# Attention with a ring of three PSUM banks for turned scores and turned results, TensorE and the DMA queue without loops

## The chip, the cores and the metric

The kernel runs on one core of a Trainium2 chip. The core has five engines with a queue each: TensorE (PE in the profile, its weight loads PEld), VectorE (DVE), ScalarE (ACT), GpSimd (POOL) and SyncE (SP), which here only issues DMAs. They meet through semaphores. PSUM is the memory that TensorE writes: 8 banks of 128 partitions x 512 float32. The metric is the device time of one execution in microseconds (us).

## The reference, cut to what matters

The input `x` is (8 batches, 1024 rows, 256 columns). The first stage, a selective scan with a layer norm, is not touched by the change. The second stage is this, per batch:

```
qkv = (x @ W_qkv + b_qkv).reshape(B, S, 3, 16, 16)         # 16 heads of 16 columns
q, k, v = qkv[:, :, 0], qkv[:, :, 1], qkv[:, :, 2]
attn = softmax(einsum('bqhd,bkhd->bhqk', q, k) / sqrt(16), axis=-1)
attn_out = einsum('bhqk,bkhd->bqhd', attn, v).reshape(B, S, 256)
gate = softmax(x @ W_gate + b_gate)                         # 8 experts, the two best count
expert_out = einsum('bsd,edf->bsef', x, W_experts) + b_experts
moe_out = einsum('bsef,bse->bsf', expert_out, combine)
x = layernorm(x + attn_out + moe_out)
```

## The kernel before

The kernel has two phases. The scan phase takes the first 1880 us. The attention phase goes through the 8 batches; for each batch there are 16 heads (`heads`) and then the experts of the next batch (`experts`), in which the maxima of heads 0 and 1 and the layer norm of the batch before are worked in.

The softmax needs each query's greatest score first. So each head's scores are computed twice. The *scores* (`scores`, L1244) have queries on the partitions; VectorE reduces a tile of 128 queries x 1024 keys to its negated maximum (`take_max`, L1588), in tiles qt = 0 to 7. They go to two pairs of banks, 0-1 and 2-3. The maxima are split in a high and a low half (`split_max`), TensorE turns them into rows (`turn_max`, L1253), ScalarE copies them (`take_max` there, L1476) to `m_rows`, and SyncE writes them by four DMAs into two extra rows of the stacked queries (`max_rows`, L1165). The *turned scores* (`scores_t`, L1261) have keys on the partitions and the maximum already subtracted, by those rows. For each tile kt of 128 keys there are two of 512 queries. ScalarE takes the exponential of each (`exp_unit`, L1463) into `probs`, and TensorE multiplies these with the values, four tiles later (`weigh_v`, L1274, accumulated over the tiles in bank 6). ScalarE copies the sums (`take_o`, L1470), TensorE turns them (`turn_o`, L1286), and VectorE divides by the row sum (`normalise`, L1595 and L1597).

The order on each engine is written out by hand. In `step`, TensorE does for each kt: turned scores half 0, scores of head h + 2 (half 1), turned scores half 1, scores of head h + 2 (half 0), then the value product; behind kt = 3 `turn_max` of head h + 1, behind kt = 6 `turn_o` of head h - 1. Heads 14 and 15 have no scores of a later head; TensorE does the projections of the next batch there (`qk_proj`, L1306). VectorE normalises head h - 1 behind reduction 7 of each step.

Banks: turned scores half 0 go to bank 4 and half 1 to bank 5, so each waits for the exponential of the tile before. Bank 7 holds turned maxima and turned results in turn, guarded by `s_nm` (normalised) and `s_mr` (rows taken). Experts use banks 4, 5 and 6 from their ninth unit on (`EBANK`), and the last two units are 30 (bank 4) and 31 (bank 5).

TensorE runs `heads(b)` and `experts(b + 1)` in a hardware loop of 7 passes; the last `heads` stands behind it. SyncE has a loop over batches with one over heads within it. ScalarE's and VectorE's instructions are written out without loops. SyncE stores a batch's output (`store_out`) in the pass of that batch, and the next pass begins with the rows of head 0.

Of the kernel before, what the change touches and what calls it, by code (L numbers as in the profile page):

```python
# [20 lines left out]
ALU = mybir.AluOpType  # L21
# [940 lines left out]
def attention_phase(nc, d):  # L962
    with ExitStack() as ctx:
# [152 lines left out]
        TERMS = tuple((k, w, x) for k in range(KH) for w, x in ((0, 0), (0, 1), (1, 0)))  # L1116
        block = ctx.enter_context(nc.Block())

        @block.sync
        def _(sp):  # L1120
# [68 lines left out]
            with sp.Fori(0, HEADS) as h:  # L1189
# [43 lines left out]
        def _(pe):  # L1233
# [15 lines left out]
            def turn_max(b, h, normalised):  # L1249

                pe.wait_ge(s_nm, normalised + 1)
                pe.wait_ge(s_mp, b * HEADS + h + 1)
                pe.transpose(ps[0:2 * TT, 7, 0:P], m_parts[:, :, :].rearrange("p c t -> p (c t)"), ident[:, :]).then_inc(s_mt, 1)  # L1253

            def scores_t(b, h, kt, half):
# [4 lines left out]
                pe.wait_ge(s_p, g * (2 * TT) + (2 * kt + half + 1))  # L1260
                pe.matmul(ps[:, 4 + half, :], head(k_st, half, QM, h, kt * P, P),  # L1261
# [16 lines left out]
            def turn_o(b, h, turned=False):  # L1278
# [44 lines left out]
            def step(b, h, before, ahead, front):  # L1323
# [3 lines left out]
                for kt in range(TT):  # L1327
# [8 lines left out]
                    if turned and kt == 3:  # L1336
                        turn_max(b, h + 1, b * HEADS + h - 1 if before else b * HEADS)
                    if before and kt == 6:
                        turn_o(b, h - 1, turned)
# [3 lines left out]
            def heads(b, more):  # L1343
                used(b, EU - 2)
                used(b, EU - 1)
# [20 lines left out]
            def experts(b):  # L1366
                for t in range(4, TT):
                    v_proj(b, t)
                for t in range(TT):
                    for e2 in range(E // 2):  # L1370
# [11 lines left out]
                        if u in EARLY:  # L1382
# [6 lines left out]
                            if unit == TT + 2:  # L1389
                                turn_max(b, 0, b * HEADS)  # L1390
# [38 lines left out]
            with pe.Fori(0, NB - 1) as b:  # L1429
# [5 lines left out]
        def _(act):  # L1435
# [23 lines left out]
            def exp_unit(b, h, kt, half):  # L1459
# [3 lines left out]
                act.activation(probs[:, kt, half * HALF:(half + 1) * HALF], ps[:, 4 + half, :], ACT.Exp,  # L1463
# [8 lines left out]
            def take_max(b, h):  # L1472
# [3 lines left out]
                act.activation(m_rows[:, :], ps[0:2 * TT, 7, 0:P], ACT.Copy).then_inc(s_mr, 1)  # L1476
# [67 lines left out]
        def _(dve):  # L1544
# [45 lines left out]
            def normalise(b, h):  # L1590
                g = b * HEADS + h
                o = ps[:, 7, 0:2 * P].rearrange("p (i j c) -> p i j c", i=2, c=VC)
# [280 lines left out]
```

## Time and profile before

| | us |
|---|---|
| median of 3 runs | 4060.7 (4050.56 to 4066.61) |
| profiled execution, its time | 4066.41 |
| its span, first to last instruction | 4064.6 |
| TensorE busy | 3655.7 (90%) |
| VectorE busy | 3444.0 (85%) |
| ScalarE busy | 2643.3 (65%) |
| GpSimd busy | 1667.9 (41%) |

The shares are averages over two unlike phases, and matmuls are pipelined, so that a busy TensorE is not one at its peak. The timeline gives each instruction's start and duration, and in brackets how long its engine had been idle and which instruction of which engine released it. "issue" is a wait for which the profile shows no releaser. A row with a count greater than one merges neighbours.

### The profile page before, as it was taken

The numbers are of one execution on the slowest core, as the hardware profiler recorded it, in microseconds if no ns is written. First come the engines' busy times: TensorE is split into PE (matmuls) and PEld (weight loads), VectorE is DVE, ScalarE is ACT, GpSimd is POOL, SyncE is SP. The second block draws the span as 40 slices with busy tenths as digits, with TensorE's granted clock in tenths as the row PEclk, the third lists the DMA queues.
The fourth block names the chain that finished last, engine by engine and source line by source line (L and its number), as shares of the span: only waits on it lengthen the run. The fifth ranks groups of instructions, "written<-read, shape, count | busy, mean of one in ns | idle before, by whom it ended". The sixth has DMA issues, their size and how long they took to land. (4 is left out here: it accounts for less than half of the span.)

```text
span 4064.6 us, 125440 instructions
## 1 busy us (share of the span) xinstructions
PE 3655.7 (90%) x52170; PEld 1663.7 (41%) x52170; DVE 3444.0 (85%) x3617; ACT 2643.3 (65%) x3895; POOL 1667.9 (41%) x1054
## 2 busy tenths in 40 slices
PE   6989999898989999893899999998999989999997
PEld 3545455554545455552323324233232332332422
DVE  5899999999899999986797896877978879689786
ACT  4666656566666657561396694875957849669498
POOL 4777777777777777785200202002011020010200
PEclk8999999999999999997899999998999999989999
DMA  3544445344444444351603306015051060420600
GB/s 94 137 112 116 122 103 145 101 122 116 128 111 129 113 110 135 96 132 58 94 2 57 49 2 94 13 30 77 2 81 26 7 99 2 62 45 2 94 2 12
DMA packets 145136, 308.02 MB, mean 76 GB/s; under 512 B 24456, under 2 KB 64016, under 8 KB 144336
## 3 DMA queue, kind: packets, MB, share of 16 engines
q1 hardware_dynamic: 144592, 299.94, 33.0%
q8 instruction: 442, 7.24, 0.8%
q14 instruction: 102, 0.84, 0.1%
HBM read 230.66 MB, written 35.13 MB: 65 GB/s over the span
## 5 line engine op out<-in xcount | busy, mean ns | idle before, releaser
L350 POOL TENSOR_TENSOR z<-z,c_rep 128x1024 f32<-128x1024 f32 x512 | 1357.4, 2667 | 456.1 <-DVE z L864 450.6
L1463 ACT ACTIVATE probs<-ps,e_scale 128x512 f32<-128x512 f32 x2048 | 1275.7, 682 | 240.2 <-PE ps L1261 197.1
L1588 DVE TENSOR_REDUCE neg_max<-ps 128x1 f32<-128x1024 f32 x1024 | 1222.8, 1220 | 132.0 <-PE ps L1244 125.8
L864 DVE TENSOR_TENSOR_SCAN z<-dA,ps 128x1024 f32<-128x1024 f32 x512 | 1150.2, 2273 | 130.2 <-PE ps L408 72.4
L1261 PE MATMUL ps<-q_st,k_st 50*128 50x512 f16 x2048 | 728.7, 399 | 100.5 <-ACT probs L1463 41.4
L705 ACT ACTIVATE dA<-rep,a_rep 128x1024 f32<-128x1024 f32 x512 | 574.2, 1144 | 331.3 <-DVE z L864 327.6
L408 PEld LDWEIGHTS ps<-diag,u_t 64*64 64x64 f32 x32768 | 542.1, 138 | 428.4 <-issue 428.2
L408 PE MATMUL ps<-diag,u_t 64*64 64x64 f32 x32768 | 605.3, 225 | 114.2 <-DVE z L864 87.7
L1244 PE MATMUL ps<-k_st,q_st 48*128 48x512 f16 x2048 | 697.8, 399 | 3.7 <-DVE neg_max L1588 3.5
L1274 PE MATMUL ps<-probs,v_h 128*32 128x256 f32 x8192 | 658.2, 396 | 0.0
L1230 POOL COPY v_h<-v_all 128x80 f32 (+1 forms) x256 | 62.0, 244 | 1412.2 <-PE ps L1274 1412.2
L427 PE MATMUL ps<-z,eye 128*64 128x512 f32 x2048 | 504.8, 613 | 3.8 <-POOL z L350 2.4
L1261 PEld LDWEIGHTS ps<-q_st,k_st 50*128 50x128 f16 x2048 | 182.5, 93 | 697.1 <-ACT probs L1463 580.4
L1224 POOL TENSOR_TENSOR x_in<-x_in,probs 128x256 f32<-128x256 f32 x256 | 191.4, 748 | 450.3 <-ACT probs L1521 438.7
L1379 PE MATMUL ps<-w_e,x1T 128*128 128x512 f16 x1536 | 366.3, 394 | 10.2 <-DVE acc L1721 10.2
L1521 ACT ACTIVATE probs<-ps,comb_s 128x256 f32<-128x256 f32 x256 | 106.5, 470 | 266.7 <-PE ps L1379 219.8
L1274 PEld LDWEIGHTS ps<-probs,v_h 128*32 128x32 f32 x8192 | 168.6, 108 | 247.0 <-issue 219.6
L1379 PEld LDWEIGHTS ps<-w_e,x1T 128*128 128x128 f16 x1536 | 148.3, 101 | 210.3 <-issue 33.5
L427 PEld LDWEIGHTS ps<-z,eye 128*64 128x64 f32 x2048 | 126.4, 138 | 248.2 <-issue 223.5
L1244 PEld LDWEIGHTS ps<-k_st,q_st 48*128 48x128 f16 x2048 | 175.4, 93 | 41.3 <-issue 25.9
L439 PE MATMUL ps<-w_io,s_res 128*128 128x256 f32 x576 | 137.4, 388 | 1.3 <-DVE s_res L845 1.3
L364 PE MATMUL ps<-xT,w_res 128*128 128x512 f32 x256 | 128.5, 625 | 0.0
(189 smaller groups left out, 3192.1 us busy)
## 6 DMA issues: line engine op xcount, KB each, us to landing
c_rep<-c_scratch SPq DMA_DIRECT2D x512, 256.0 KB, 4.0
rep<-delta SPq DMA_DIRECT2D x128, 256.0 KB, 5.0
q_st<-qk_halves SPq DMA_DIRECT2D x192, 128.0 KB, 10.3
k_st<-qk_halves SPq DMA_DIRECT2D x192, 128.0 KB, 10.9
qk_halves<-qk_parts SPq DMA_DIRECT2D x32, 512.0 KB, 10.7
x_nat<-in_x SPq DMA_DIRECT2D x9, 1024.0 KB, 10.1
x_rows<-x_nat SPq DMA_DIRECT2D x9, 1024.0 KB, 6.4
xT<-in_xT SPq DMA_DIRECT2D x8, 1024.0 KB, 7.2
```

Source lines behind the costliest of these rows:

```text
L350: pool.tensor_tensor(z[:, k % ZR, :], z[:, k % ZR, :], c_rep[:, slot, :], ALU.mult).then_inc(s_zc, 1)
L408: mm = pe.matmul(ps[q * QD:(q + 1) * QD, 2 + 2 * (k % 2) + r, i * TB:(i + 1) * TB], u_t[rows, i, m * P + j * QD:m * P + (j + 1) * QD], dia ...
L427: mm = pe.matmul(ps[j * QD:(j + 1) * QD, half, :], eye[:, :], z[:, (grp * QN + j) % ZR, half * HALF:(half + 1) * HALF], start=False, stop= ...
L705: act.activation(dA[:, k % AR, :], rep[:, slot, :], ACT.Exp, scale=a_rep[:, m, j, g:g + 1]).then_inc(s_da, 1)
L864: dve.tensor_tensor_scan(z[:, k % ZR, :], dA[:, k % AR, :], pair(1 + k % 2), 0.0, ALU.mult, ALU.add).then_inc(s_z, 1)
L1224: pool.tensor_tensor(to, to, scaled[:, i % 2, e, :], ALU.add).then_inc(s_pa, 1)
L1244: mm = pe.matmul(ps[:, 2 * (qt % 2) + half, :], head(q_st, half, QR, h, qt * P, P), head(k_st, half, QR, h, half * HALF, HALF), start=True ...
L1261: pe.matmul(ps[:, 4 + half, :], head(k_st, half, QM, h, kt * P, P), head(q_st, half, QM, h, half * HALF, HALF), start=True, stop=True).the ...
L1274: mm = pe.matmul(ps[VC * j:VC * (j + 1), 6, 0:n], v_h[:, kt, :], probs[:, kt, j * n:(j + 1) * n], start=(kt == 0), stop=(kt == TT - 1), sk ...
L1379: mm = pe.matmul(ps[:, EBANK[u], :], x1T[:, x, k, t * P:(t + 1) * P], w_e[:, w, k, e2 * 2 * H:(e2 + 1) * 2 * H], start=(i == 0), stop=(i = ...
L1463: act.activation(probs[:, kt, half * HALF:(half + 1) * HALF], ps[:, 4 + half, :], ACT.Exp, scale=e_scale[:, h:h + 1]).then_inc(s_p, 1)
L1588: dve.tensor_reduce(neg_max[:, qt:qt + 1], pair(qt % 2), AX.X, ALU.max, negate=True).then_inc(s_mx, 1)
```

## The change

Three banks, 4, 5 and 7, become one ring. Its users are numbered in the order in which TensorE writes them: the turned scores of each tile ("probs"), the turned maxima behind kt = 3 ("rows") and the turned results behind kt = 6 ("sums"). User n takes bank `RING[n % 3]` and waits for what empties the bank of user n - 3: an exponential, the copy of the rows, or the normalisation. The first three users of a batch wait for the experts' units 30 and 31 and for the rows of head 0. On VectorE the normalisation moves from behind reduction 7 to behind reduction 6, the last `join` (the sum of the two expert accumulators) from the end of the experts to behind the first reduction of the heads, and the wait for the stored output from the start of the heads to the first normalisation. TensorE's and SyncE's loops are written out. SyncE issues the rows of the next batch's head 0 ahead of the store of the output. ScalarE only reads other banks.

```diff
@@ attention_phase @@
+        RING = (4, 5, 7)
+        USERS = []
+        for h in range(HEADS):
+            for kt in range(TT):
+                USERS += [("probs", h, 2 * kt), ("probs", h, 2 * kt + 1)]
+                if kt == 3 and h < HEADS - 1:
+                    USERS.append(("rows", h + 1, 0))
+                if kt == 6 and h:
+                    USERS.append(("sums", h - 1, 0))
+        SLOT = {user: n for n, user in enumerate(USERS)}
+
+        def ring_bank(user):
+
+            return RING[SLOT[user] % 3] if user in SLOT else 7
...
@@ SyncE @@
-            with sp.Fori(0, NB - 1) as b:
-                max_rows(b, 0)
+            max_rows(0, 0)
+            for b in range(NB - 1):
                 sp.wait_ge(s_fa, (b + 1) * TT)
                 load_x(b + 1)
-                with sp.Fori(1, HEADS) as h:
+                for h in range(1, HEADS):
                     max_rows(b, h)
...
+                max_rows(b + 1, 0)
                 store_out(b)
-            with sp.Fori(0, HEADS) as h:
+            for h in range(1, HEADS):
                 max_rows(NB - 1, h)
...
@@ TensorE @@
-            def turn_max(b, h, normalised):
-
-                pe.wait_ge(s_nm, normalised + 1)
+            def ring_free(b, user):
+
+
+                n = SLOT[user] - len(RING)
+                if n == -3:
+                    used(b, EU - 2)
+                elif n == -2:
+                    used(b, EU - 1)
+                elif n == -1:
+                    pe.wait_ge(s_mr, b * HEADS + 2)
+                else:
+                    kind, h, i = USERS[n]
+                    if kind == "probs":
+                        pe.wait_ge(s_p, (b * HEADS + h) * (2 * TT) + i + 3)
+                    elif kind == "rows":
+                        pe.wait_ge(s_mr, b * HEADS + h + 2)
+                    else:
+                        pe.wait_ge(s_nm, b * HEADS + h + 2)
+
+            def turn_max(b, h):
+
+                if h:
+                    ring_free(b, ("rows", h, 0))
+                else:
+                    pe.wait_ge(s_nm, b * HEADS + 1)
                 pe.wait_ge(s_mp, b * HEADS + h + 1)
...
-                pe.wait_ge(s_p, g * (2 * TT) + (2 * kt + half + 1))
-                pe.matmul(ps[:, 4 + half, :], head(k_st, half, QM, h, kt * P, P),
+                ring_free(b, ("probs", h, 2 * kt + half))
+                pe.matmul(ps[:, ring_bank(("probs", h, 2 * kt + half)), :], head(k_st, half, QM, h, kt * P, P),
...
-                if turned:
-                    pe.wait_ge(s_mr, g + 4)
+                user = ("sums", h, 0)
                 pe.wait_ge(s_o, g + 2)
-                pe.wait_ge(s_nm, g + 1)
+                if h < HEADS - 1:
+                    ring_free(b, user)
+                else:
+                    pe.wait_ge(s_nm, g + 1)
+                    pe.wait_ge(s_p, (g + 1) * (2 * TT) + 2)
                 for i in range(2):
-                    mm = pe.transpose(ps[:, 7, i * P:(i + 1) * P], o_sb[:, i * P:(i + 1) * P], ident[:, :])
+                    mm = pe.transpose(ps[:, ring_bank(user), i * P:(i + 1) * P], o_sb[:, i * P:(i + 1) * P], ident[:, :])
...
             def heads(b, more):
-                used(b, EU - 2)
-                used(b, EU - 1)
                 pe.wait_ge(s_stk[1], (b + 1) * (12 * 3 * 16))
...
-            with pe.Fori(0, NB - 1) as b:
+            for b in range(NB - 1):
                 heads(b, True)
                 experts(b + 1)
...
@@ VectorE @@
+                if h == 0:
+                    dve.wait_ge(s_done, (b + 1) * 16)
                 dve.wait_ge(s_ot, g + 2)
...
                     take_max(b, h + PRE, qt, True)
-                    if qt == TT - 1 and before:
+                    if qt == 0 and not before:
+                        join(b, TT - 1)
+                    if qt == 6 and before:
                         normalise(b, h - 1)
 
             def heads(b, more):
-                dve.wait_ge(s_done, (b + 1) * 16)
                 step(b, 0, False)
...
-                join(TT - 1)
```

TensorE, a steady head, from the turning of the maxima (L1253, now L1292) to the next round. Before:

```order
L1253 MATMUL ps<-ident,m_parts 16x128 [waits max_parts_done,head_normalised]
L1260 REGISTER_ALU
L1261 MATMUL ps<-q_st,k_st 128x512 [waits probs_ready]
L1243 REGISTER_ALU
L1244 MATMUL ps<-k_st,q_st 128x512 [waits max_done]
L1260 REGISTER_ALU
L1261 MATMUL ps<-q_st,k_st 128x512 [waits probs_ready]
L1244 MATMUL ps<-k_st,q_st 128x512
```

Now (turned scores are L1300, scores L1261):

```order
L1292 MATMUL ps<-ident,m_parts 16x128 [waits max_parts_done,probs_ready]
L1300 MATMUL ps<-q_st,k_st 128x512 [waits probs_ready]
L1261 MATMUL ps<-k_st,q_st 128x512 [waits max_done]
L1300 MATMUL ps<-q_st,k_st 128x512 [waits probs_ready]
L1261 MATMUL ps<-k_st,q_st 128x512
L1313 MATMUL ps<-probs,v_h 32x256 [waits o_taken,v_head_ready,probs_ready]
L1313 MATMUL ps<-probs,v_h 32x256 x3
L1300 MATMUL ps<-q_st,k_st 128x512 [waits max_rows_ready]
```

The register operations are gone, the turned maxima wait for an exponential instead of a normalisation, and the first turned scores of round 5 wait for the copy of the rows. At the end of the head, in the same way, the turned scores wait for a normalisation:

```order
L1313 MATMUL ps<-probs,v_h 32x256 x3
L1300 MATMUL ps<-q_st,k_st 128x512 [waits head_normalised,max_rows_stacked]
L1261 MATMUL ps<-k_st,q_st 128x512 [waits max_done]
L1300 MATMUL ps<-q_st,k_st 128x512 [waits probs_ready]
L1261 MATMUL ps<-k_st,q_st 128x512
```

VectorE, from the last reductions of a steady head on. Before:

```order
L1588 TENSOR_REDUCE neg_max<-ps 128x1 [waits scores_ready] x7
L1595 RECIPROCAL r_sum<-ps 128x8 [waits o_transposed]
L1597 TENSOR_TENSOR att<-ps,r_sum 128x2x4x16 [waits row_sum_inverted]
L1573 TENSOR_SCALAR m_rest<-neg_max 128x8 [waits max_done]
L1574 TENSOR_SCALAR m_hi<-neg_max 128x8
L1588 TENSOR_REDUCE neg_max<-ps 128x1 [waits scores_ready,max_split_step]
```

Now:

```order
L1628 TENSOR_REDUCE neg_max<-ps 128x1 [waits scores_ready] x6
L1637 RECIPROCAL r_sum<-ps 128x8 [waits o_transposed]
L1639 TENSOR_TENSOR att<-ps,r_sum 128x2x4x16 [waits row_sum_inverted]
L1628 TENSOR_REDUCE neg_max<-ps 128x1 [waits scores_ready]
L1613 TENSOR_SCALAR m_rest<-neg_max 128x8 [waits max_done]
L1614 TENSOR_SCALAR m_hi<-neg_max 128x8
L1628 TENSOR_REDUCE neg_max<-ps 128x1 [waits scores_ready,max_split_step]
```

A reduction now stands between the normalisation and the split of the maxima.

## Rows read from the trace of the kernel before

**Rows 1.** Timeline of ScalarE, steady head: start us, us, instruction, count [idle before <- releaser].
```profile
2102.72 2.43 ACT L1463 ACTIVATE probs<-ps,e_scale 128x512 f32<-128x512 f32 x4 [0.20 <-PE ps L1261]
2105.36 1.26 ACT L1463 ACTIVATE probs<-ps,e_scale 128x512 f32<-128x512 f32 x2 [0.20 <-PE ps L1261]
...
2107.50 1.83 ACT L1463 ACTIVATE probs<-ps,e_scale 128x512 f32<-128x512 f32 x3
```

**Rows 2.** Timeline of VectorE, the same head of batch 0.
```profile
2100.34 1.22 DVE L1588 TENSOR_REDUCE neg_max<-ps 128x1 f32<-128x1024 f32 x1 [0.26 <-PE ps L1244]
...
2102.19 1.22 DVE L1588 TENSOR_REDUCE neg_max<-ps 128x1 f32<-128x1024 f32 x1
...
2103.48 3.48 DVE L1588 TENSOR_REDUCE neg_max<-ps 128x1 f32<-128x1024 f32 x3
...
2108.68 2.39 DVE L1588 TENSOR_REDUCE neg_max<-ps 128x1 f32<-128x1024 f32 x2 [0.32 <-PE ps L1244]
2111.33 1.23 DVE L1588 TENSOR_REDUCE neg_max<-ps 128x1 f32<-128x1024 f32 x1 [0.26 <-PE ps L1244]
```

**Rows 3.** Timeline of TensorE, the same head.
```profile
2102.30 0.39 PE L1261 MATMUL ps<-q_st,k_st 50*128 50x512 f16 x1
...
2103.47 0.39 PE L1261 MATMUL ps<-q_st,k_st 50*128 50x512 f16 x1
...
2110.28 0.44 PE L1286 MATMUL ps<-ident,o_sb 128*128 128x128 f32 x2
2110.65 0.39 PE L1261 MATMUL ps<-q_st,k_st 50*128 50x512 f16 x1
```

**Rows 4.** Timeline of ScalarE, heads 14 and 15 of the last batch.
```profile
4025.53 0.38 ACT L1470 ACTIVATE o_sb<-ps 128x256 f32<-128x256 f32 x1
...
4036.55 0.38 ACT L1470 ACTIVATE o_sb<-ps 128x256 f32<-128x256 f32 x1
```

**Rows 5.** Timeline of VectorE, head 0 and start of head 1, last batch.
```profile
3867.65 1.22 DVE L1588 TENSOR_REDUCE neg_max<-ps 128x1 f32<-128x1024 f32 x1 [0.16 <-PE ps L1244]
...
3869.04 1.22 DVE L1588 TENSOR_REDUCE neg_max<-ps 128x1 f32<-128x1024 f32 x1 [0.16 <-PE ps L1244]
...
3875.95 1.22 DVE L1588 TENSOR_REDUCE neg_max<-ps 128x1 f32<-128x1024 f32 x1 [0.35 <-PE ps L1244]
...
3877.55 1.23 DVE L1588 TENSOR_REDUCE neg_max<-ps 128x1 f32<-128x1024 f32 x1
```

**Rows 6.** Windows, same head 0: stretch, us, busy (count) by engine, granted clock, DMA.
```profile
3865.00:3875.00 10.00, 9.63 (x49) 1.78 (x49) 8.00 (x9) 8.24 (x14) 0.00 (x0) 0.50 0.00 0
```

**Rows 7.** Waits, heads 14 and 15 of batch 1: in total, times, longest.
```profile
PE ps L1261 <- ACT probs L1463: 1.2, 6, 0.2
```

**Rows 8.** Timeline where heads start (batch 1, batch 7); waits of the whole phase.
```profile
2279.89 1.52 POOL L1224 TENSOR_TENSOR x_in<-x_in,probs 128x256 f32<-128x256 f32 x2 [1.85 <-ACT probs L1521]
...
2284.25 0.60 PE L1261 MATMUL ps<-q_st,k_st 50*128 50x512 f16 x1 [5.39 <-issue]
...
2284.94 5.42 ACT L1463 ACTIVATE probs<-ps,e_scale 128x512 f32<-128x512 f32 x8 [5.20 <-issue]
...
3862.65 0.37 PE L1261 MATMUL ps<-q_st,k_st 50*128 50x512 f16 x1 [0.97 <-issue]
...
3864.26 5.42 ACT L1463 ACTIVATE probs<-ps,e_scale 128x512 f32<-128x512 f32 x8 [1.72 <-POOL x_in L1224]
...
PE ps L1261 <- issue: 33.9, 7, 5.6
```

**Rows 9.** Waits of the whole attention phase.
```profile
PE ps L1319 <- issue: 21.5, 7, 3.4
```

**Rows 10.** Timeline of SyncE, steady head; waits for these rows, attention phase.
```profile
2107.74 2.90 SPq L1165 DMA_DIRECT2D q_st<-m_rows  x4
...
PEld ps L1261 <- DMA q_st<-m_rows: 7.5, 14, 0.5
```

**Rows 11.** DMA queues in the attention phase: packets, MB, share of 16 engines.
```profile
q8 instruction: 153, 2.51, 0.5%
```

More of the change, by code:

```diff
@@ L1247, in scores @@
                     mm.then_inc(s_sc, 1)
-            def turn_max(b, h, normalised):
-                pe.wait_ge(s_nm, normalised + 1)
+            def ring_free(b, user):
[19 more added lines that the diff above has]
+                    pe.wait_ge(s_nm, b * HEADS + 1)
                 pe.wait_ge(s_mp, b * HEADS + h + 1)
-                pe.transpose(ps[0:2 * TT, 7, 0:P], m_parts[:, :, :].rearrange("p c t -> p (c t)"), ident[:, :]).then_inc(s_mt, 1)
+                pe.transpose(ps[0:2 * TT, ring_bank(("rows", h, 0)), 0:P], m_parts[:, :, :].rearrange("p c t -> p (c t)"), ident[:, :]).then_inc(s_mt, 1)
             def scores_t(b, h, kt, half):
@@ L1336, in step @@
                     if turned and kt == 3:
-                        turn_max(b, h + 1, b * HEADS + h - 1 if before else b * HEADS)
+                        turn_max(b, h + 1)
                     if before and kt == 6:
-                        turn_o(b, h - 1, turned)
+                        turn_o(b, h - 1)
                     for work, args in front.get(kt, ()):
@@ L1389, in experts @@
                             if unit == TT + 2:
-                                turn_max(b, 0, b * HEADS)
+                                turn_max(b, 0)
                     if t == 1:
@@ L1462, in exp_unit @@
                 act.wait_ge(s_pv, g * TT + (kt + 1))
-                act.activation(probs[:, kt, half * HALF:(half + 1) * HALF], ps[:, 4 + half, :], ACT.Exp,
+                act.activation(probs[:, kt, half * HALF:(half + 1) * HALF], ps[:, ring_bank(("probs", h, 2 * kt + half)), :], ACT.Exp,
                                scale=e_scale[:, h:h + 1]).then_inc(s_p, 1)
@@ L1475, in take_max @@
                 act.wait_ge(s_md, g * 64 + 16)
-                act.activation(m_rows[:, :], ps[0:2 * TT, 7, 0:P], ACT.Copy).then_inc(s_mr, 1)
+                act.activation(m_rows[:, :], ps[0:2 * TT, ring_bank(("rows", h, 0)), 0:P], ACT.Copy).then_inc(s_mr, 1)
             def step(b, h, before, turned):
@@ L1649, in take_v, with join @@
                                          op0=ALU.mult, op1=ALU.add).then_inc(s_ve, 1)
+            def join(b, t):
+                dve.wait_ge(s_pa, b * EU + (4 * t + 8))
+                dve.wait_ge(s_ea, b * (EU // 2) + (2 * t + 2))
+                if t == 2:
+                    dve.wait_ge(s_eba, (b + 1) * 5)
+                dve.tensor_tensor(acc[:, t, :], acc[:, t, :], x_in[:, t, :], ALU.add).then_inc(s_fa, 1)
             def experts(b, late):
@@ L1687, in experts @@
                                   ALU.mult).then_inc(s_cbs, 1)
-                def join(t):
-                    dve.wait_ge(s_pa, b * EU + (4 * t + 8))
-                    dve.wait_ge(s_ea, b * (EU // 2) + (2 * t + 2))
-                    if t == 2:
-                        dve.wait_ge(s_eba, (b + 1) * 5)
-                    dve.tensor_tensor(acc[:, t, :], acc[:, t, :], x_in[:, t, :], ALU.add).then_inc(s_fa, 1)
                 for t in range(TT):
@@ L1727, in experts @@
                     if t:
-                        join(t - 1)
+                        join(b, t - 1)
                     if t == 2:
```

6 lines of the change are left out of this document (3 added, 3 removed).

## The prediction

> **What bounds the kernel now.** I read the timeline of one steady head engine by engine, then the places where two stages meet, then the waits. A steady head lasts 10.99 us: VectorE starts the same reduction at 2100.34 and at 2111.33 [rows 2]. I call a "round" one tile of keys: two turned score matmuls (L1261), two score matmuls of the head two further on (L1244), and the four-quarter value product (L1274). A head has eight rounds.
>
> No engine is full in that time. I work out a floor for each, from the stretches in which it is not held.
>
> - ScalarE: exponentials that follow one another start (2.43 - 0.70) / 3 = 0.58 us apart (the 0.70 is the rest of the last one; four of them took 2.43) [rows 1]. Between 2105.36 and 2107.50 it did three exponentials and the two small copies (o_sb, m_rows) in 2.14 us, 0.41 more than three exponentials need [rows 1]. Floor 16 x 0.577 + 0.41 = 9.64 us.
> - VectorE: three reductions took 3.48 us and two took 2.39 [rows 2]. With 1.22 for the last one that is a pitch of 1.13 and 1.17. The four small operations between 2100.34 and 2102.19 add 1.85 - 1.13 = 0.72, the two of the next stage 0.16 (2102.19 to 2103.48). Floor 9.04 + 0.88 = 9.92 us.
> - TensorE: a round took 1.17 us where nothing was late (2102.30 to 2103.47), and the turning of results takes 0.37 (2110.28 to 2110.65) [rows 3]. With about 0.2 for the turning of the maxima: 8 x 1.17 + 0.6 = 9.9 us.
>
> So 1 us per head is lost in hand-overs. Each of the two banks of turned scores can be refilled only after the exponential that reads it, TensorE is in order, and behind the refill stands the value product. Then ScalarE idles 0.20 us, twice in those rows, waiting for L1261 [rows 1], and VectorE 0.32 and 0.26 us waiting for L1244 [rows 2]. The best witness is the last batch: its last two heads have no scores ahead and no reductions, yet o_sb follows o_sb after 11.02 us [rows 4]. It is the loop between exponential and refill that costs this, not VectorE.
>
> **The change part by part.**
>
> *Ring of three banks.* A refill waits for the exponential three users back instead of two, so there is one exponential (0.58 us) of slack, half of TensorE's round of 1.17 us. The ScalarE to TensorE loop is then off the path. What is late next is VectorE, and its own work grows: the normalisation moves from behind reduction 7 to behind reduction 6. The split of the maxima then stands behind a fresh reduction, where it cost 1.60 - 1.13 = 0.47 us (3875.95 to 3877.55) [rows 5]; the normalisation alone costs between 0.72 - 0.47 = 0.25 and 0.72, I take 0.45, since its two operations depend on each other. VectorE's new floor: 8 x 1.13 + 0.47 + 0.45 + 0.16 = 10.12 us, and with the pitch of 1.17 it is 10.44. I take 10.30, the middle. The move pays for itself: turning the results delays TensorE by 0.37 us just when VectorE is busy for 0.45 with the normalisation. Gain 10.98 - 10.30 = 0.68 us for heads 1 to 13 of 8 batches: 104 x 0.68 = 71 us. Bounds: 0 and 104 x 0.86 = 89.
>
> The added wait: the first turned score of head h+1 now waits for the normalisation of head h-1. Behind it on TensorE stand the scores of that round, and VectorE waits for these. Normalisation ends about 0.5 us behind reduction 6; the scores are needed only behind reduction 7 and the split, 1.6 us later, and from the start of a round to the reduction of its scores the trace has 0.68 us (2110.65 to 2111.33) [rows 2, 3]. Hidden, with almost 1 us to spare.
>
> *Head 0 of each batch* runs at a granted clock of 0.50, the 1.2 GHz level, for 10 us or so [rows 6]. Its first four rounds have no value product; VectorE's reductions stood 1.39 us apart there (3867.65, 3869.04) [rows 5]. One more bank brings them to 1.17 to 1.2: 4 x 0.2 x 8 = 6 us. Behind that TensorE itself is the limit at this clock, and nothing is gained. Bounds 0 and 10.
>
> *Heads 14 and 15.* Last batch: 11.02 down to ScalarE's 9.64, twice: 2.8 us. In the seven others TensorE also carries the next batch's projections; its own idle time on exponentials is 1.2 us [rows 7], and I take all of it: 8.4. Together 11 us, bounds 5 and 25 (ScalarE waits far longer there, but for an engine that is working).
>
> *TensorE without a loop.* At the start of batch 1 TensorE idled 5.39 us and nothing in the trace released it [rows 8]. Batch 7, which comes by falling out of the loop with the same order of DMA issues, had 0.97. Over the whole phase there are seven such pauses, 33.9 us, so the six starts of batches 1 to 6 have (33.9 - 0.97) / 6 = 5.5 us each: this is the jump back to the loop's head. What would be late next is known from batch 7: GpSimd's last addition. It ended at 2279.89 + 1.52 = 2281.41, and ScalarE overwrites its operand, so the first exponential could start at 2281.45 instead of 2284.94 [rows 8]. 6 x 3.5 = 21 us. Bounds: 15, and 27 if the shorter pause also keeps the clock up.
> The Trainium skill ("Advanced Engine Details and Errata", Control Flow Timing) prices a compare and branch at about 108 ns; by that this term would be 6 x 0.1, under 1 us, and the total 89. Its page "Runtime: NRT & Kernel Launch" (Instruction fetch mechanics) says that a taken branch out of the current window has to fetch its target first, and the idle 5.39 us agree with the second.
>
> *Rows of the first maxima ahead of the output's store.* In batch 7 these rows were behind the store too, and TensorE was not held. The work that hides them is the last two expert units. 0 us; were that cover gone, it would be some us for each of 7 batches. The join of the last expert sum moves behind a reduction, and GpSimd has ended by then; the wait for the stored output moves two heads later: both 0.
>
> *Code.* The straight code changes where instruction blocks end. Today TensorE stops once in each of the seven loop passes in the middle of a projection (L1319), between two matmuls that wait for nothing, 21.5 us in all and 3.4 at most [rows 9]. These 22 us may vanish or double. I take no change, bounds -22 and +22.
>
> Sum: 71 + 6 + 11 + 21 = 109 us. The profiled execution took 4066.4 us (span 4064.6), 5.7 above the median of 4060.7. From its own time that gives 3957; scaled to the median, **3952 us**, 2.7% less.
>
> **Rivals.**
>
> *A: the rows of maxima become late.* SyncE issues four DMAs from 2107.74 over 2.90 us [rows 10], and TensorE opens the next head at 2110.65 + 1.17 = 2111.8, 4.1 us after the first issue. Fourteen heads already waited for the landing, 7.5 us in all [rows 10]. With a head of 10.3 us the distance shrinks by up to 0.6. For it: the slack is near nothing. Against: without loops the register operations between the four issues are gone too, which brings the last one forward. If it bites, heads stay at 10.7: 104 x 0.28 + 6 + 11 + 21 = 67, so 3994.
>
> *B: the ring brings nothing*, since VectorE's hand-over with TensorE (two pairs of banks, unchanged) is what really sets the head. Then 21 us for the loop remain: 4040. Against it: the last two heads, 11.02 us with no reductions at all [rows 4].
>
> *C: the pause of 5.4 us is not the jump* but something that comes with each batch, and stays: 3952 + 21 = 3973. Against: batch 7.
>
> *D, the slower side: straight code starves TensorE.* Its place is each instruction block: the instruction queue moved 153 blocks in this phase [rows 11]. If a block that is fetched while the stacked heads are loaded comes late, TensorE stops, as in rows 9. The change turns slower once the 153 blocks cost 109 / 153 = 0.7 us each on average; at 1 us the time is 4060.7 - 109 + 153 = 4105. Against: the loop body itself is straight code with as many blocks per pass, and it shows one such stop in it.
> The Trainium skill ("Runtime: NRT & Kernel Launch", Instruction fetch mechanics) says that crossing a block's end is mostly hidden; the single stop per pass, 3 us, is where it is not.
>
> **How the numbers follow.** Forecast 0.62, A 0.18, C 0.08, B 0.07, D 0.05. With every term at its good end together the time would be 4060.7 - 89 - 10 - 25 - 27 - 22 = 3888; I hold that all of them come so for less than 1 in 10, and start at 3925. The range 3925 to 4003 takes in the forecast, A and C; it leaves out B, D and the edges, under 2 in 10. Within 0.5% (20 us, about what a measurement tells from no change) lies only part of B: faster 0.91, same 0.04, slower 0.05.
>
> **What would show it.** Steady heads: o_sb to o_sb 10.2 to 10.45 us; ScalarE's 0.20 us gaps on L1261 gone or moved; VectorE with at most 0.2 us of idle time per head. If heads stand at 10.7 with TensorE waiting for q_st<-m_rows, it is A; at 11.0, B. Start of batches 1 to 6: no idle time over 2.5 us on TensorE, first exponential 0.1 us behind GpSimd's last addition; else C. Stops of 3 us on TensorE without a releaser: seven or so; thirty or more is D. Wrong altogether I would be if VectorE shows a gap in every round with TensorE busy in that time: then TensorE's real floor is above 9.9.

## The result and the profile after

| | before | after |
|---|---|---|
| median | 4062.68 (4050.56 to 4066.61, 4 runs) | 3899.66 (3898.46 to 3907.31, 4 runs) |
| profiled execution, its time | 4066.41 | 3907.31 |
| span | 4064.6 | 3905.5 |

The ratio is 0.9608, 95% interval 0.9583 to 0.9632: 163 us less, where 109 were forecast. The time lies below the range that I gave (3925 to 4003).

The scan phase is the same code everywhere, yet the first exponential of the attention phase starts anywhere from 2010.3 to 2028.2 us in the profiled executions below. So beside the medians I use the length of the attention phase itself, from the first exponential to the last copy of results (o_sb): 2021.8 us before (2021.8 to 4043.5), 1860.2 after (2024.2 to 3884.4), 161.6 less. Cut at the first exponential of each head and at the last o_sb of each batch, it comes apart like this (heads 1 to 13 are the steady ones; their length in the table is the usual one from o_sb to o_sb):

| stretch | before | after | difference | forecast |
|---|---|---|---|---|
| steady head, o_sb to o_sb (104 of them) | 10.98 | 10.11 | -91 in all | -71 |
| head 0, mean | 12.76 | 11.96 | -6 | -6 |
| heads 14 and 15, seven batches / the last | 35.40 / 23.17 | 33.98 / 21.31 | -12 | -11 |
| experts: last o_sb to the next batch's first exponential, sum of seven | 505.3 | 453.5 | -52 | -21 |

First, VectorE in a steady head of the changed kernel (timeline: start, duration, instruction, count, and in brackets the idle time before; L1628 is the reduction, L1637 and L1639 the normalisation, L1613 to L1619 the split of the maxima).

```profile
2098.51 6.94 DVE L1628 TENSOR_REDUCE neg_max<-ps 128x1 f32<-128x1024 f32 x6
2105.37 0.20 DVE L1637 RECIPROCAL r_sum<-ps 128x8 f32<-128x8 f32 x1
2105.60 0.29 DVE L1639 TENSOR_TENSOR att<-ps,r_sum 128x128 f32<-128x128 f32 x1
2105.81 1.21 DVE L1628 TENSOR_REDUCE neg_max<-ps 128x1 f32<-128x1024 f32 x1
2107.06 0.17 DVE L1613 TENSOR_SCALAR m_rest<-neg_max 128x8 f32<-128x8 f32 x1
2107.14 0.17 DVE L1614 TENSOR_SCALAR m_hi<-neg_max 128x8 f16<-128x8 f32 x1
2107.34 1.23 DVE L1628 TENSOR_REDUCE neg_max<-ps 128x1 f32<-128x1024 f32 x1
2108.48 0.16 DVE L1618 CAST m_parts<-m_hi 128x8 f32<-128x8 f16 x1
2108.55 0.16 DVE L1619 TENSOR_TENSOR m_parts<-m_rest,m_hi 128x8 f32<-128x8 f32 x1
2108.62 4.61 DVE L1628 TENSOR_REDUCE neg_max<-ps 128x1 f32<-128x1024 f32 x4
```

No row has a bracket: VectorE never waits in this head, and its gaps of 0.26 and 0.32 us [rows 2] are gone. The period is 2108.62 - 2098.51 = 10.11 us. The reductions follow one another after (6.94 - 1.22) / 5 = 1.144 us.

TensorE and ScalarE in the same head (L1300 turned scores, L1503 exponentials):

```profile
2102.42 0.39 PE L1300 MATMUL ps<-q_st,k_st 50*128 50x512 f16 x1
...
2103.53 0.39 PE L1300 MATMUL ps<-q_st,k_st 50*128 50x512 f16 x1
```
```profile
2101.53 0.69 ACT L1503 ACTIVATE probs<-ps,e_scale 128x512 f32<-128x512 f32 x1
2102.11 0.25 ACT L1516 ACTIVATE m_rows<-ps 16x128 f16<-16x128 f32 x1
2102.27 2.99 ACT L1503 ACTIVATE probs<-ps,e_scale 128x512 f32<-128x512 f32 x5
2105.43 5.99 ACT L1503 ACTIVATE probs<-ps,e_scale 128x512 f32<-128x512 f32 x10 [0.17 <-PE ps L1300]
```

A round of TensorE takes 1.11 us (2103.53 - 2102.42) where nothing is late, not the 1.17 of [rows 3]. ScalarE is held by TensorE once, for 0.17 us, where it had several gaps of 0.20 [rows 1].

Waits of the changed kernel's attention phase (who waited for whom: us in total, times, longest):

```profile
PEld ps L1300 <- DMA q_st<-m_rows: 44.2, 105, 1.0
DVE neg_max L1628 <- PE ps L1261: 41.1, 57, 1.4
```
```profile
PE ps L1437 <- issue: 6.1, 7, 0.9
```

TensorE's only wait without a releaser is one of 0.9 us per batch. The six pauses of 5.4 to 5.6 us at the head of a batch [rows 8] and the seven stops in the projection [rows 9] are gone. TensorE's weight load now waits for the rows of the maxima in 105 heads where it waited in 14 [rows 10].

The start of batch 1 in the changed kernel:

```profile
2264.32 0.39 PE L1300 MATMUL ps<-q_st,k_st 50*128 50x512 f16 x1 [0.61 <-ACT probs L1561]
...
2264.42 1.52 POOL L1241 TENSOR_TENSOR x_in<-x_in,probs 128x256 f32<-128x256 f32 x2 [1.86 <-ACT probs L1561]
...
2265.98 4.73 ACT L1503 ACTIVATE probs<-ps,e_scale 128x512 f32<-128x512 f32 x8 [1.71 <-POOL x_in L1241]
```

The first exponential starts 0.04 us behind GpSimd's last addition (2264.42 + 1.52), as forecast [rows 8].

### The profile page after: what moved, and what is told of

The parts are those of the page before. It is cut to its first block, busy times and chain, and to the rows that moved or that the text cites. A ratio compares the mean times of both kernels' runs of the same rounds, so it can differ in the third digit from the quotient of the medians.

```text
span 3905.5 us, 121218 instructions
## 1 busy us (share of the span) xinstructions
PE 3588.3 (92%) x52170; PEld 1623.6 (42%) x52170; DVE 3426.8 (88%) x3617; ACT 2617.0 (67%) x3895; POOL 1667.7 (43%) x1054
## 4 chain that ended last, share of the span: by engine, by line
PE 23%; ACT 11%; issue 9%; DVE 7%; POOL 0%; DMA 0%; ACTq 0%; SPq 0%; DVEq 0%; POOLq 0%
ACT probs L1503 9%; PE ps L1313 6%; PE ps L1300 5%; PE ps L1419 4%; DVE neg_max L1628 3%; PE ps L1348 2%; PE ps L1261 2%; PE ps L1328 1%; PE ps L1361 1%; ACT o_sb L1510 1%; PE ps L1445 1%; DVE acc L1764 1%; ACT m_rows L1516 1%; DVE diag_b L1786 1%; DVE x1T L1594 1%
## 5 line engine op out<-in xcount | busy, mean ns | idle before, releaser
L1503 ACT ACTIVATE probs<-ps,e_scale 128x512 f32<-128x512 f32 x2048 | 1241.8, 688 | 132.9 <-PE ps L1300 117.8
L1628 DVE TENSOR_REDUCE neg_max<-ps 128x1 f32<-128x1024 f32 x1024 | 1204.2, 1218 | 45.5 <-PE ps L1261 41.1
L1300 PE MATMUL ps<-q_st,k_st 50*128 50x512 f16 x2048 | 676.5, 393 | 29.9 <-ACT probs L1503 17.6
L1261 PE MATMUL ps<-k_st,q_st 48*128 48x512 f16 x2048 | 581.1, 393 | 3.6 <-DVE neg_max L1628 3.5
L427 PE MATMUL ps<-z,eye 128*64 128x512 f32 x2048 | 512.8, 622 | 3.8 <-POOL z L350 2.7
L1300 PEld LDWEIGHTS ps<-q_st,k_st 50*128 50x128 f16 x2048 | 159.5, 94 | 467.9 <-ACT probs L1503 240.6
L1261 PEld LDWEIGHTS ps<-k_st,q_st 48*128 48x128 f16 x2048 | 133.7, 93 | 60.7 <-issue 25.8
L619 ACT ACTIVATE u_t<-ps 128x1024 f32<-128x1024 f32 x32 | 32.6, 1018 | 146.3 <-PE ps L382 146.3
```

The source lines that it names most:

```text
L427: mm = pe.matmul(ps[j * QD:(j + 1) * QD, half, :], eye[:, :], z[:, (grp * QN + j) % ZR, half * HALF:(half + 1) * HALF], start=False, stop= ...
L1261: mm = pe.matmul(ps[:, 2 * (qt % 2) + half, :], head(q_st, half, QR, h, qt * P, P), head(k_st, half, QR, h, half * HALF, HALF), start=True ...
L1300: pe.matmul(ps[:, ring_bank(("probs", h, 2 * kt + half)), :], head(k_st, half, QM, h, kt * P, P), head(q_st, half, QM, h, half * HALF, HAL ...
L1628: dve.tensor_reduce(neg_max[:, qt:qt + 1], pair(qt % 2), AX.X, ALU.max, negate=True).then_inc(s_mx, 1)
```

## Experiments

"Attention" is the phase's length as above; differences are taken on it, since the medians also carry the scan phase.

| kernel | median us | ratio to before (95%) | attention | steady head |
|---|---|---|---|---|
| before | 4057 to 4063 | 1 | 2021.8 | 10.98 |
| after | 3899.66 | 0.9608 | 1860.2 | 10.11 |
| e1 before, loops written out | 4017.28 | 0.9905 (0.9886 to 0.9923) | 1977.3 | 11.03 |
| e2 after, TensorE in a loop | 3937.71 | 0.9699 (0.9683 to 0.9715) | 1896.5 | 10.19 |
| e3 before, half a block of filler | 4021.57 | 0.9908 (0.989 to 0.9927) | 1975.8 | 10.99 |
| e4 after, late normalisation | 4046.34 | 0.9967 (0.9955 to 0.9978) | 2010.2 | 11.31 |
| e5 before, a whole block of filler | 4056.96 | 0.9998 (0.9985 to 1.0012) | 2019.8 | 10.99 |
| e6 before, early normalisation | 4057.36 | 1.0 (0.9985 to 1.0014) | 2024.4 | 10.98 |
| e7 after, split on GpSimd | 3878.52 | 0.9558 (0.9528 to 0.9587) | 1840.1 | 9.93 |
| e8 after, SyncE as before | 3915.22 | 0.9646 (0.9615 to 0.9677) | 1874.8 | 10.19 |
| e9 after, store first | 3901.06 | 0.9607 (0.9591 to 0.9624) | 1860.2 | 10.11 |
| e10 after, half a block of filler | 3908.84 | 0.9621 (0.9604 to 0.9638) | 1861.9 | 10.11 |
| e11 e2 and half a block of filler | 3916.60 | 0.9644 (0.9629 to 0.9659) | 1878.7 | 10.18 |
| e12 e7, rows a round earlier | 3895.73 | 0.9598 (0.9584 to 0.9611) | 1857.5 | 10.13 |

### Is it the loop or the place of the code?

**e1**, the kernel before with TensorE's and SyncE's loops written out (TensorE's is shown; SyncE's three are alike).

```diff
-            with pe.Fori(0, NB - 1) as b:
+            for b in range(NB - 1):
```


> The kernel before with TensorE's and SyncE's loops written out and nothing else changed (two banks, all orders as before). Theory 1: the 52 us that the change saved outside the heads belong to the loop alone: six jumps back (6 x 3.5 = 21 us), seven stops of 3.1 us in a projection because the code block that comes next is fetched behind the loads of the stacked heads (22 us), and the two passes in which the clock stayed low longer (8 us). Then 4062.7 - 50 = 4012 us (4005 to 4022), heads unchanged at 10.98 us from o_sb to o_sb. Rival: only the jumps belong to the loop, and the stops went because the ring shifted the heads against the loads: 4040 us, with seven stops of 3 us still there.

4017.3 us, as the first theory had it: 44.5 us less attention (the experts' stretches fell from 505.3 to 456.6, while heads became 0.05 us longer, which I can't explain). Writing out the loops takes both the pauses and the stops away, so this run can't tell which of the two does what.

**e3**, the kernel before with nothing changed but 64 small matmuls ahead of the loop, 128 TensorE instructions with their weight loads.

```diff
+            for i in range(64):
+                pe.matmul(ps[:, 7, 0:64], b_one[:, 0:P], b_one[:, 0:64], start=True, stop=True)
             pe.wait_ge(s_qs, 6)
             for k in range(KH):
```


> The kernel before, loop kept, with 64 small matmuls (128 instructions) put ahead of the loop where TensorE waits 46 us for the weights; they only move where the 16 KB code blocks end. Theory 1: the block that was asked for 3 us after the loads began is now asked for before them, and the stops of 3.1 us in the projection vanish or move: 4062.7 - 22 = 4041 (4030 to 4050). Rival (the stop comes with each pass of a loop wherever the blocks end): unchanged, 4063 +- 4, L1319 still stopped seven times.

A miss (4021.6, where 4041 were expected), and the one that taught most. With all loops in place it gained 46.0 us of attention, as much as e1. Its waits of TensorE without a releaser are these, against 33.9 at the head of a batch [rows 8] and 21.5 in the projection [rows 9]:

```profile
PE ps L1261 <- issue: 18.2, 7, 3.0
```

The stops in the projection are gone (21.5 us), and the pause at the jump back is 2.7 to 3.0 instead of 5.5 us, which takes the row of pauses from 33.9 to 18.2.

**e5**, the same with 128 matmuls, 256 instructions: one block of 16 KB, of the size that the instruction queue q8 moves (2.51 MB in 153 packets [rows 11]). In the attention phase of the kernel before, the median distance between two blocks of TensorE's code is 247 of its instructions, as far as the trace records them.

```diff
-            for i in range(64):
+            for i in range(128):
```


> The kernel before, with 128 small matmuls (256 TensorE instructions, one instruction block of 16 KB) ahead of the loop; the run with 64 of them (half a block) took 4021.6 against 4059.9. Theory: what counts is where in the loop's code the blocks end, and a shift by a whole block changes nothing: the seven stops at the projection (about 3.1 us each) and the long pauses of 5.5 us at the jump come back, 4063 us (4055 to 4070). Rival: the filler helped in another way (a clock that is raised earlier, or merely other addresses of the loop's head), and any filler helps: 4022 us (4012 to 4035).

Everything came back, as the theory had it (waits of TensorE in its attention phase):

```profile
PE ps L1261 <- issue: 34.7, 7, 6.0
```
```profile
PE ps L1319 <- issue: 20.0, 7, 3.4
```

So filler as such does nothing: half a block was worth 46 us, a whole block 2. What counts is where the loop's code lies in its blocks.

**e2**, the changed kernel with TensorE's batches in a loop, and **e11**, e2 with e3's 64 matmuls.

```diff
-            for b in range(NB - 1):
+            with pe.Fori(0, NB - 1) as b:
                 heads(b, True)
                 experts(b + 1)
```


> The changed kernel with TensorE's batches back in a hardware loop of seven passes (ring, VectorE's order and SyncE without loops stay). Theory 1: heads stay at 10.11 us, six jumps come back with 3.5 us each, and the stop in the projection only if a block's end falls into the first part of the loads: 3900 + 21 = 3921 without it, 3943 with it. Rival (register waits of a looped TensorE slow the heads): heads at 10.3 us or more, 3940 to 3970 with no stop in the projection.

> The changed kernel with TensorE's batches in a hardware loop (3937.7 us, pauses of 5.8 us at six jumps) and the 64 small matmuls ahead of it. Theory: the pause at a jump back is a chain of block fetches, and its length depends on where the loop's head and end lie in their blocks; shifted by half a block the pause falls from 5.8 to about 3 us, as in the kernel before: 6 x 2.8 = 17 us less, 3921 us (3912 to 3928). So a loop in a good place would cost about 20 of these 38 us. Rival: the pause belongs to the jump itself: 3938 us.

The loop costs 36.3 us of attention in e2 and 18.6 in e11. The median of e11 was as expected; that of e2 is 17 us above the 3921 that I expected without a stop, since the experts' stretches took 28 us more instead of 21, and the steady heads 6. The pauses (e2, then e11) make the difference between the two, and neither kernel has a stop in the projection:

```profile
PE ps L1300 <- issue: 34.6, 6, 7.4
```
```profile
PE ps L1300 <- issue: 15.9, 6, 2.8
```

Of e11's 18.6, the experts' stretches have 8.5 and the steady heads nearly 7; the rest lies in head 0.

**e10**, the changed kernel with the 64 matmuls (the diff is e3's).

> The changed kernel with the same 64 small matmuls (128 TensorE instructions, half a block) ahead of the batches that took 38 us off the kernel before. Theory: in straight code a batch has 3925 TensorE instructions, 85 more than a multiple of 256, so that each batch meets other block ends, and all but none of them stops TensorE: a shift changes nothing that can be measured, 3900 us (3895 to 3908). Rival: the changed kernel was merely lucky in its block ends, as the kernel before was unlucky: 3915 us or more, with stops of 3 us.

Attention is 1.7 us longer, no more than kernels with the same steady heads differ by (e5 2.0 below before, e6 2.6 above). The median, 3908.8, lies 0.8 above the range that I had given; most of the 9 us by which it rose isn't in the attention phase, which in the profiled execution began 3.7 us later. No stop appeared: at this second place, too, the straight code runs without one.

How a block comes late can be read from the traces. In the kernel before, near the end of batch 1, TensorE around the stop:

```profile
2478.15 2.41 PE L1319 MATMUL ps<-w_vg,x1T 128*128 128x264 f16 x20
2483.68 1.04 PE L1319 MATMUL ps<-w_vg,x1T 128*128 128x264 f16 x4 [3.11 <-issue]
```

and of its DMA queues from 2480 to 2484 the row of the instruction queue, which is one block (packets, MB, share of 16 engines):

```profile
q8 instruction: 1, 0.02, 2.8%
```

In the 30 us before, from 2450 to 2480, the same view has no row for q8 at all; what stands there is the load of the stacked heads (the rows of loads: how many, KB each, median us from issue to landing):

```profile
q1 hardware_dynamic: 1861, 3.18, 69.4%
...
q_st<-qk_halves SPq DMA_DIRECT2D x12, 128.0 KB, 10.3
k_st<-qk_halves SPq DMA_DIRECT2D x12, 128.0 KB, 11.0
```

The block arrived while TensorE stood still; 540 TensorE instructions had started since the block before. In the changed kernel, too, one block comes in 28 us of the same load (2430 to 2458), but only 465 instructions fall between it and the block before, and TensorE works through it:

```profile
q1 hardware_dynamic: 2118, 3.52, 99.5%
q8 instruction: 1, 0.02, 0.4%
```
```profile
2448.75 10.52 PE L1419 MATMUL ps<-w_e,x1T 128*128 128x512 f16 x48
```

All passes agree. In the seven of the kernel before and the seven of e5, 492 to 544 instructions start between two blocks at this load, and TensorE stops in each, for 2.8 to 3.4 us; in the changed kernel, e1, e3 and e10 it is never more than 471, and TensorE doesn't stop.

At the jump it is the chain of blocks that counts. During the pause of 5.39 us of the kernel before (2278.5 to 2284.3) q8 moved two blocks, during the first pause of e3, 3.01 us (2275.8 to 2279.2), one, in this order:

```profile
q8 instruction: 2, 0.03, 2.1%
```
```profile
q8 instruction: 1, 0.02, 2.3%
```

The same holds for the first pauses of e2 (5.39 us, two) and e11 (2.79 us, one).

I did not change the loads, so that the late block waits behind them is read, not shown by a run. That the place of the code in its blocks decides is shown by e3 and e5.

### What does the ring need?

**e4**, the changed kernel with the normalisation behind reduction 7 again.

```diff
-                    if qt == 6 and before:
+                    if qt == TT - 1 and before:
```


> The changed kernel with the normalisation back behind reduction 7. Theory 1: TensorE's first turned scores of a head wait for it, it ends 0.5 us behind reduction 7, the fill takes 0.7 us, and VectorE has only the split (0.2 us more) to do in that time: heads 10.4 us, 104 x 0.3 = +31, 3931 us (3920 to 3950). Rival: VectorE's smaller sum of work decides (9.92 instead of 10.12 us per head): 3880 us.

A miss by 115 us: nearly all of the gain is lost (150 of 162 us of attention), and heads of 11.31 us are longer than before the change. TensorE at the start of a head, VectorE, and the wait over the phase:

```profile
2120.90 0.37 PE L1300 MATMUL ps<-q_st,k_st 50*128 50x512 f16 x1 [1.31 <-DVE att L1639]
```
```profile
2119.09 1.23 DVE L1628 TENSOR_REDUCE neg_max<-ps 128x1 f32<-128x1024 f32 x1 [0.33 <-PE ps L1261]
...
2120.46 0.29 DVE L1639 TENSOR_TENSOR att<-ps,r_sum 128x128 f32<-128x128 f32 x1
...
2121.65 1.23 DVE L1628 TENSOR_REDUCE neg_max<-ps 128x1 f32<-128x1024 f32 x1 [0.75 <-PE ps L1261]
```
```profile
PE ps L1300 <- DVE att L1639: 136.1, 104, 1.3
```

The first turned score of a head shares its bank with the turned results. TensorE, in order, stands 1.31 us, and the scores behind it come late for VectorE (0.75 idle): 104 x (11.31 - 10.11) = 125 of the 150 us. Most of the rest is the clock: 13 single heads take 12.7 us, and in each of them the granted clock stands at its lower level, 1.2 GHz, for 3.4 us. The first of them and the head behind it (windows: us, busy by engine, clock, DMA share, GB/s):

```profile
2304.60:2317.30 12.70, 11.22 (x101) 2.88 (x99) 10.47 (x15) 10.06 (x19) 0.45 (x2) 0.87 0.00 1
2317.30:2328.60 11.30, 9.90 (x101) 2.88 (x99) 9.87 (x15) 9.84 (x19) 0.51 (x3) 1.00 0.01 2
```

In the steady heads of the kernels before and after the granted clock is 1.00 throughout. What e4 adds to bring it down, the run doesn't show.

**e6**, the kernel before with only that move on VectorE.

```diff
-                    if qt == TT - 1 and before:
+                    if qt == 6 and before:
```


> The kernel before, where only VectorE's normalisation moves from behind reduction 7 to behind reduction 6; two banks and loops stay. Theory (three banks are what frees ScalarE's and TensorE's round, and the move is needed only so that the ring's first wait of a head is short): heads stay at 10.9 to 11.0 us, 4060 us (4040 to 4070). Rival (VectorE's order is what counts, and the ring only looks like it): heads fall to 10.5 or less, 4010 us or less.

4057.4, heads 10.98: nothing, as the theory had it. Alone the move is worth 0, the ring without it 11.31 instead of 10.98, both together 10.11. They are one edit. The other two moves on VectorE, of the last join and of the wait for the stored output, were not run alone.

### What bounds the changed kernel?

**e7**, the four operations of the split on GpSimd, with two alternating buffers for the maxima. GpSimd's loops over batches and heads are written out with it, so the run changes two things; VectorE's timeline is where the first of them shows.

```diff
+            def split_max(b, h):
...
+                pool.tensor_scalar(m_rest[:, :], neg_max[:, h % 2, :], down, None, ALU.mult).then_inc(s_ms, 1)
+                pool.tensor_scalar(m_hi[:, :], neg_max[:, h % 2, :], down, None, ALU.mult).then_inc(s_ms, 1)
...
+                    if 0 < h < HEADS - 1:
+                        split_max(b, h + 1)
...
-                if before and qt < 2:
-                    split_max(b, h - 1, qt)
```


> The changed kernel, where GpSimd splits the maxima (four small operations of VectorE per head, 0.39 + 0.14 = 0.53 us in the changed kernel's timeline) into two alternating buffers. Theory: VectorE, which is never idle in a steady head of 10.11 us, bounds it now; without the split it needs 9.58, and ScalarE's 9.64 is next: heads of 9.65 to 9.75, 104 x 0.4 = 42 us less, 3858 us (3845 to 3875). Rival 1: TensorE's round is the bound, heads stay at 10.1, 3900 us. Rival 2: the rows of the maxima, on which TensorE's weight load already waits in 105 heads, land too late with shorter heads or with a slower GpSimd: heads of 9.9 to 10.3, 3880 to 3920 us.

The fastest kernel here: 3878.5 us, 20.1 of attention below the changed kernel, half of what I expected. VectorE has a gap again, and TensorE has no idle time except behind the turned maxima (L1308; turned scores are L1316, scores L1277):

```profile
2096.52 3.51 DVE L1628 TENSOR_REDUCE neg_max<-ps 128x1 f32<-128x1024 f32 x3 [0.30 <-PE ps L1277]
```
```profile
2105.23 0.28 PE L1308 MATMUL ps<-ident,m_parts 128*16 128x128 f32 x1
2105.43 0.39 PE L1316 MATMUL ps<-q_st,k_st 50*128 50x512 f16 x1
...
2106.00 0.39 PE L1316 MATMUL ps<-q_st,k_st 50*128 50x512 f16 x1 [0.18 <-ACT probs L1519]
```

TensorE: 8 rounds of 1.11 are 8.88, turning the results 0.37 and 0.08 behind it, turning the maxima 0.20, and 0.34 + 0.07 lost behind them, where a turned score waits for the exponential three users back: 9.94, measured 9.93. So VectorE did bound the changed kernel, but TensorE with the ring's wait stood only 0.18 us behind it.

**e12**, e7 with the turned maxima behind kt = 2, to take that 0.41 away.

```diff
-                    if turned and kt == 3:
+                    if turned and kt == 2:
                         turn_max(b, h + 1)
```


> The kernel with the split on GpSimd (3878.5 us, heads of 9.93 us, TensorE without a gap but for the waits for an exponential), where the turned maxima stand behind kt = 2 instead of kt = 3 in the ring, and ScalarE copies them at kt = 3. Theory: in it TensorE loses 0.33 us behind the turned maxima because the copy of the results (o_sb) and the ring's third user fall on the same place; apart from one another that goes, and heads take 9.65 to 9.8: 104 x 0.2 = 21 us less, 3858 us (3850 to 3868). Rival: the ring has the same one exponential less of slack wherever the maxima stand, and heads stay at 9.93: 3878 us (3872 to 3882).

A miss: 17.4 us more attention than e7. ScalarE now copies the rows just ahead of the results, and the value product waits for the latter:

```profile
2106.92 0.25 ACT L1532 ACTIVATE m_rows<-ps 16x128 f16<-16x128 f32 x1
...
2107.65 0.36 ACT L1526 ACTIVATE o_sb<-ps 128x256 f32<-128x256 f32 x1
```
```profile
2108.15 0.64 PE L1329 MATMUL ps<-probs,v_h 128*32 128x256 f32 x8 [0.22 <-ACT o_sb L1526]
```
```profile
PE ps L1329 <- ACT o_sb L1526: 23.2, 106, 0.6
```

The last row is that wait over the phase; in e7 it came once, with 0.6 us.

### SyncE's part

**e8**, the changed kernel with SyncE's loops and order of before; **e9**, with the store of the output first, no loops.

```diff
-                max_rows(b + 1, 0)
                 store_out(b)
+                max_rows(b + 1, 0)
```


> The changed kernel with SyncE's loops over batches and heads as before, and the rows of the next batch's head 0 again behind the output's store. SyncE's four issues of rows take 2.90 us with the loop and 2.43 without. Theory: the wait of TensorE's weight load for the rows is hidden by 0.5 us or more in a steady head, and the rows of head 0 are covered by the last expert units: 3901 us (3897 to 3908). Rival (rows are at the edge): each of 104 heads is 0.2 to 0.5 us longer, 3920 to 3950 us.

> The changed kernel with only the output's store back ahead of the rows of the next batch's head 0 on SyncE; no loops. Theory (the last two expert units hide these rows, and the order is worth nothing): 3900 us (3896 to 3904). Rival (they were late behind the store): 1 to 3 us for each of seven batches, 3907 to 3921 us.

e9: 0.0 us of attention, so the order is worth nothing, as the theory had it. e8: 14.6 us more, between what the theory and the rival had. Now TensorE itself waits for the rows, not only its weight load (e8):

```profile
PEld ps L1299 <- DMA q_st<-m_rows: 70.0, 105, 0.9
```
```profile
PE ps L1299 <- DMA q_st<-m_rows: 18.4, 91, 0.4
```

Steady heads (10.19 instead of 10.11) make 9 us of it, the experts' stretches 5. The rows do stand at the edge, and only the straight code of SyncE keeps them inside it: its four issues take 2.42 us in the changed kernel where [rows 10] has 2.90, and e8 has 2.90 again.

```profile
2418.75 2.42 SPq L1181 DMA_DIRECT2D q_st<-m_rows  x4
```

## Why the prediction was wrong, point by point

Two terms of the sum failed, the first in its mechanism, the second in its size; between them they have nearly all of the 53 us that the forecast missed.

**The step that failed: "Code. ... I take no change".** The stops in the projection, 21.5 us [rows 9], went altogether, and with them about 8 us of longer experts. In the two passes of before that took 75 us for the experts instead of 71, the mean granted clock was lower (windows, with the columns as in e4):

```profile
2475.50:2550.50 75.00, 64.84 (x303) 29.26 (x300) 54.82 (x115) 24.47 (x57) 24.62 (x34) 0.89 0.67 98
2213.60:2285.00 71.40, 60.59 (x303) 28.20 (x301) 55.49 (x115) 24.40 (x57) 24.52 (x34) 0.95 0.70 104
```

TensorE's mean clock is 0.89 in the first of these rows and 0.95 in the second. With two levels, 2.4 and 1.2 GHz (1.00 and 0.50), that is 16.5 us (75 x 0.11 / 0.5) at the lower one in the first and 7 in the second. A stretch of the changed kernel, which takes 64.7 to 65.4 us in all seven:

```profile
2443.30:2507.90 64.60, 60.58 (x305) 28.09 (x303) 56.16 (x115) 24.36 (x56) 23.99 (x33) 0.97 0.73 107
```

Here it is 4 us. That the lower clock made the passes longer is read from these rows; no run changed it alone. I had -22 as the bound and held both signs equal. They were not: the row showed one stop at one place in every pass, which is an unlucky place. e3 took all seven stops away without an edit to the loop, e5 brought them back, and straight code met none at either of its two places (the changed kernel and e10).

**"TensorE without a loop", 21 us.** The mechanism was right (first exponential behind GpSimd, no pause over 2.5 us), and the experts' 52 us are 21.5 of stops, some 21 here (6 x 3.5, as forecast), and a rest of 9 that I put down to the clock. But 5.5 us is not "the jump back": the same jump takes at most 3.0 in e3. By the Trainium skill ("Runtime: NRT & Kernel Launch", Instruction fetch mechanics) a taken branch out of the window fetches its target first. The trace agrees in kind, and adds that the pause was 5.4 us where two blocks were fetched in it and 3.0 where it was one. Rival C is out.

**"Ring of three banks", 71 us.** Right in mechanism, too small: the head is the VectorE floor that I had worked out, 10.12, and I took 10.30 because a pair of reductions stood 1.17 us apart [rows 2]. The pair was no pitch: six reductions on end have 1.144, near the 1.13 of the longer one of my two samples. 104 x 0.87 comes to 91, just outside the bound of 89. TensorE's floor of 9.9 went wrong in the same way: its round of 1.17 us was a single one, and the changed kernel has 1.11. "The move pays for itself" was far too weak: it is the condition of the ring (e4, e6). Rival B is out.

**The added wait, "hidden, with almost 1 us to spare".** Right with the early normalisation: no wait for it is seen. e4 shows its price with the late one, 1.31 us of TensorE in every steady head.

**Head 0, 6 us, and heads 14 and 15, 11 us.** 6.4 and 11.8: right.

**"Rows of the first maxima", 0.** Right (e9); the two zeros beside it, for the join and the stored output, have no run of their own.

**Rival A** had the mechanism, not the outcome: in 105 heads the weight load waits for the rows, yet the steady heads stand at VectorE's floor. I named SyncE's register operations only as an argument against A and gave their removal no value; it is worth 14.6 us (e8), 9 of them in the steady heads, so that without it the ring would have brought about 82 and not 91. **Rival D** did not come: TensorE's waits without a releaser are down to 0.9 us per batch.

Sum: forecast 109, measured 162 (attention). Of the 53 missing, 20 are the steady head, 31 the experts with their stops and the clock. I had worked out that all terms at their good ends together give 3888, and called it less than 1 in 10. For the steady head the trace already had the answer, in the longer of the two samples; for the stops it had the seven rows at one place, and e3 was the run to ask.

## What to carry to other kernels

A stop without a releaser at one place of every loop pass may be a block of code that comes late: move the code (filler of half a block is a test of a line or two) before you take the loop apart, and if the stop goes, count it as a gain. A bank ring shared by several kinds of user must have each user's release ahead of the next user's turn: look at what else stands behind the waiting instruction on TensorE, and test the ring and the reordering both apart and together. A pitch is read from a long run of back-to-back instructions, never from a pair.

## What the runs showed of the hardware

- Half a block (128 TensorE instructions) of filler shortened the kernel before by 46 us of attention (e3), a whole block by 2 (e5).
- A jump back on TensorE cost a mean of 2.7 us of idle time in e11 (15.9 / 6) and 5.8 in e2 (34.6 / 6), with the same loop, by its place alone.
- While 24 loads of 128 KB were under way, the next block of TensorE's code came only 28 to 32 us behind the one before in the seven passes of the kernel before, and 21 to 28 us in those of the changed kernel. With 492 to 540 instructions in the gap TensorE stopped for 2.8 to 3.4 us; with up to 471 (changed kernel, e1, e3, e10) it didn't.
- SyncE issues four small DMAs in 2.90 us from a loop and in 2.42 from straight code.
- 3.4 us at the lower level of the granted clock made a steady head of e4 1.4 us longer (12.7 instead of 11.3), in 13 heads.
- Straight code on TensorE and SyncE made a head of the old kernel 0.05 us longer (e1), straight code on TensorE one of the new 0.08 shorter (e2 against the changed kernel). That is open.
